# Two stages of a fused token model, their edge woven on one core: the last attention turns run together with the first mixing rounds

## The chip, the cores and the metric

One core of a Trainium2 chip (trn2). The time of a kernel is device microseconds of one launch, the median of several runs. The profile comes from one further execution, recorded by the hardware profiler.

## What is computed

128 images of 224x224 become 64 tokens of width 64 each (a two-level Haar transform, a resize, a linear layer); 32 text tokens are put behind them, which makes 96 tokens per image. Then four residual blocks follow, each on a layer-normed input. Cut to what matters:

```
h = concat([tok(x), txt], axis=1)                    # 128 x 96 x 64
h = h + gated_attention(layernorm(h))                # stage A
h = h + expert_attention(layernorm(h))               # stage B
h = h + mixing(layernorm(h))                         # stage C
h = h + routed_experts(layernorm(h))                 # stage D (routing) and E (experts)

# stage B: 4 heads x 4 expert queries of width 16 over shared keys and values
s   = einsum('bnesd,bntd->bnest', q, k) * 4 + causal
qkv = einsum('bnest,bntd->bnesd', softmax(s), v)     # zeroed where the head input is 0
gs  = softmax(out @ gate_w + gate_b)                 # weights of the 4 experts
hn  = layernorm16(sum_e gs * qkv + resid)
hx  = layernorm16(fc2(relu(fc1(hn))) + hn)           # rows of width 16
out = hx * softmax(hx @ fgate_w)                     # one weight per head

# stage C: k, v, r = ln(x) @ Wk, Wv, Wr
y = wkv(w/T, u/T, k, v)                              # a scan along the 96 tokens
x = x + sigmoid(r) * y @ Wo
x = x + sigmoid(ln(x) @ Wr2) * (relu(ln(x) @ Wk2)**2 @ Wv2)
```

Everything is float32 apart from a few masks.

## The kernel before

It is written engine by engine: each engine has its own instruction stream, executed strictly in its order, and semaphores tie the streams together. All activations of all images stay on chip in `H` (96 tokens on the partitions, 128 x 64 columns), so that no stage around the change moves data in or out; the DMA share there is 0.

**Stages and turns.** Stage B takes the images in NG = 32 groups of G = 4. Stage C takes them in NR = 16 rounds of GD = 8, so round r needs the groups 2r and 2r+1 of stage B. Both are software pipelines written out with `grouped(eng, n, *stages)` (line 68): each entry of the list is a pair (lag, function), and in turn t an engine issues each function for group t - lag, in the order of the list. The last turns of stage B, 32 to 37 (there are up to 6 lags), have fewer and fewer entries: the run-out. The code uses `u`, the turn's buffer, beside `g`, the group.

**The edge.** TensorE, ScalarE, VectorE and GpSimd each end stage B and then wait for `b_h` = 32, the semaphore that VectorE raises when a group's residual has been added to `H` (line 1604). So no engine begins stage C before the last group of stage B is done. VectorE then sets constants (`c_decay` and borders, lines 1619 to 1627) and begins round 0.

**Stage B's late steps of a group**, in the order of dependence: `b_outs` (VectorE, lines 1504 and 1508), `b_pads` (GpSimd, 1278), `b_outT` (TensorE, 708), `b_outF` (ScalarE), `b_gates` (TensorE, 719), `b_gate1` (VectorE, 1516), `b_gexp` (ScalarE, 1065), `b_gate2` (VectorE), `b_weigh` (GpSimd, 1285), `b_mix` and `b_center1` (VectorE, 1541 to 1531), `b_squares1` (ScalarE, 1083), `b_var1` (VectorE, 1534), `b_pow1` (GpSimd, 1291), `b_hns` (VectorE, 1557), `b_fx` (TensorE), `b_fxFs` (ScalarE), `b_fc1s` (TensorE, 730), `b_reluF` (ScalarE, 1091), `b_h1s` (VectorE, 1562), `b_fc2s` (TensorE, 734), `b_ys` (VectorE, 1568), `b_yTs` (TensorE), `b_center2` (VectorE, 1529 to 1531), `b_squares2` (ScalarE, 1087), `b_var2` (VectorE, 1534), `b_pow2` (GpSimd, 1295), `b_fos` (VectorE, 1585 to 1587), `b_foTs` (TensorE), `b_foFs` (ScalarE), `b_fgates` (TensorE, 747), `b_w1` (VectorE, 1593), `b_wexp` (ScalarE, 1079), `b_w2` (VectorE, 1599 to 1604).

**Stage C's steps of a round**: `c_ln` (VectorE, 1645 to 1647), `c_squares` (ScalarE, 1113), `c_var` (VectorE, 1652), `c_power` (GpSimd, 1311), `c_scale1` (ScalarE, eight pieces, recorded at the helper's line 1006), `c_norm` (VectorE, 1659), `c_transpose` (TensorE, 770), `c_features` (ScalarE, 1006), `c_kvr` (TensorE, 790 to 793), `c_kvs` (ScalarE, 1006 and 1134), `c_wkv1` (VectorE, 1669 to 1673), `c_exps` (ScalarE, 1139 to 1144), `c_wkv2` (VectorE, 1684 to 1694), `c_out` (TensorE, 799), `c_resid` (VectorE, 1700 to 1710), then the second norm, the hidden layer, `c_values` (TensorE, 838) and `c_end` (VectorE, 1727 to 1729). The lags run from 0 to 4; stage C's rounds 0 to 7 are written out, 8 to 15 run in a hardware loop.

**Memory.** PSUM has 8 banks, and each stage names its own: before, stage B has the scores in 0 and 1, the turned scores (`T0_`) in 2 and 3, outputs 4 (`O_`), features 5 (`F_`), queries and gates 6 (`Q_`), the small layers 7 (`Z_`). Stage C uses all eight in the order of its names. The on-chip tiles of both stages are cut from one `arena`, where they lie on top of each other, and from `XR`.

Of the kernel before, what the change touches and what calls it, by code (L numbers as in the profile page):

```python
# [111 lines left out]
def build(nc, t_in, table, mpe, out):  # L112
    ctx = ExitStack()
    with ctx:  # L114
# [112 lines left out]
        gst = tb("gst", [NTOK, 4, G * NH])
        gd = tb("gd", [NTOK, G * NM])
        ge = tb("ge", [NTOK, G * NM])
        gs = tb("gs", [NTOK, G * NM])  # L230
# [1 line left out]
        hm = tb("hm", [NTOK, GC])
        hc = tb("hc", [NTOK, GC])
        hs = tb("hs", [NTOK, GC])
        hn = tb("hn", [NTOK, GC])
        hst = tb("hst", [NTOK, 4, G * NH])
        hcy = tb("hcy", [NTOK, GC])
        hsy = tb("hsy", [NTOK, GC])
        hsty = tb("hsty", [NTOK, 4, G * NH])
        gsty = tb("gsty", [NTOK, 4, G * NH])  # L240
        gdy = tb("gdy", [NTOK, G * NH])
        gey = tb("gey", [NTOK, G * NH])
        fxF = tb("fxF", [P, FC])
        pmF = tb("pmF", [P, FC])
        h1 = tb("h1", [P, FC])
        yF = tb("yF", [P, FC])
        fo = tb("fo", [NTOK, GC])
        foF = tb("foF", [P, FC])
        assert tb.at <= 14592
# [1769 lines left out]
```

## Time and profile before

| | us |
|---|---|
| median of 3 runs | 2515.45 (2511.88 to 2518.7) |
| the profiled execution | 2491.33 |
| its span in the profile | 2489.3 |

Busy shares of the span and instructions:

| engine | busy us | share | instructions |
|---|---|---|---|
| TensorE, matmuls | 1906.3 | 77% | 16407 |
| VectorE | 1609.2 | 65% | 5040 |
| ScalarE | 976.9 | 39% | 3150 |
| GpSimd | 1045.3 | 42% | 878 |

The page cuts the span in 40 slices of 62.2 us. The expert attention, stage B, ends in slice 24 and stage C in slice 29; the images and stage A lie before, the routing and the experts behind. Slices 23 and 24 hold the edge between stage B and stage C. The profiled execution is 24 us shorter than the median of the runs: differences are read within one trace, and set against its own time.

How the rows below are read: a line of the timeline is one instruction or several merged ones: start in us from the span's start, duration in us, engine, source line, operation, what it writes and reads, the shape; in brackets the idle time of the engine before it and who ended it. PE is TensorE, DVE VectorE, ACT ScalarE, POOL GpSimd. A row of windows gives, for a stretch, its length, then busy us (and number of instructions) of PE, of PE's weight loads, of DVE, ACT and POOL, then the granted TensorE clock as a share of full speed.

### The profile page before, as it was taken

What the parts mean: (1) busy time and instruction counts of PE and PEld (TensorE: products, weight loads), DVE (VectorE), ACT (ScalarE), POOL (GpSimd) and SP (SyncE); (2) the same over time, 40 slices, a digit from 0 to 9 for tenths busy, and PEclk for the clock granted to TensorE, in tenths of its full rate; (3) what the DMA queues carried; (4) which work ended last, traced back from release to release, by engine and by line L of the source; (5) the groups of instructions that cost most, each with busy time, mean ns of one, the idle gap of its engine ahead of it and who ended that gap; (6) DMA issues with size and microseconds to landing.
All of it is one profiled execution on the core that took longest, in us unless ns stands there. A gap on an engine that the chain in (4) does not pass through costs nothing. (4 is left out here: it accounts for less than half of the span.)

```text
span 2489.3 us, 52573 instructions
## 1 busy us (share of the span) xinstructions
PE 1906.3 (77%) x16407; PEld 1481.9 (60%) x16407; DVE 1609.2 (65%) x5040; ACT 976.9 (39%) x3150; POOL 1045.3 (42%) x878
## 2 busy tenths in 40 slices
PE   5778887899999999999999527677533332998970
PEld 2256666677777777777777415556422222887860
DVE  0035564368888888888888559999588873333223
ACT  2366664234444444444444247877322210111100
POOL 0033342023443443444433422222178784777772
PEclk9989998689999999999999557777655555555555
DMA  9910000000000000000000000000000003665526
GB/s 283 299 46 0 0 0 0 1 2 2 2 1 0 0 0 0 0 0 0 0 0 1 1 0 1 1 0 0 0 21 22 23 22 92 180 166 146 159 81 160
DMA packets 119877, 106.63 MB, mean 43 GB/s; under 512 B 62448, under 2 KB 109680, under 8 KB 118896
## 3 DMA queue, kind: packets, MB, share of 16 engines
q1 hardware_dynamic: 87024, 73.88, 11.3%
q10 hardware_dynamic: 18432, 16.79, 2.3%
q0 software_dynamic: 14336, 14.91, 1.8%
q8 instruction: 45, 0.74, 0.1%
q14 instruction: 40, 0.33, 0.0%
HBM read 78.84 MB, written 26.67 MB: 42 GB/s over the span
## 5 line engine op out<-in xcount | busy, mean ns | idle before, releaser
L1006 ACT ACTIVATE arena<-PS 128x384 f32<-128x384 f32 (+3 forms) x384 | 178.5, 483 | 570.6 <-DMA arena<-in_t_experts_dram 212.2
L1354 POOL DMA_INDIRECT expert_rows<-arena x256 | 248.4, 970 | 104.0 <-issue 77.5
L1489 DVE TENSOR_REDUCE XR<-PS 128x2 f32<-128x192 f32 (+2 forms) x768 | 173.7, 280 | 105.0 <-PE PS L645 104.8
L645 PE MATMUL PS<-arena 32*128 32x96 f32 (+2 forms) x3072 | 234.1, 285 | 0.0
L1341 POOL DMA_INDIRECT routed_rows<-XR,SLu x192 | 201.5, 1049 | 74.9 <-issue 67.3
L645 PEld LDWEIGHTS PS<-arena 32*128 32x128 f32 x3072 | 198.4, 192 | 20.7
L1042 ACT ACTIVATE XR<-PS 128x256 f32<-128x256 f32 x512 | 167.3, 380 | 67.2 <-PE PS L660 66.9
L1295 POOL TENSOR_TENSOR arena<-arena,mhalf 96x16 f32<-96x16 f32 x32 | 92.7, 2898 | 225.8 <-DVE arena L1535 225.8
L1493 DVE TENSOR_TENSOR XR<-PS,XR 128x192 f32<-128x192 f32 (+2 forms) x768 | 172.4, 278 | 0.0
L612 PE MATMUL PS<-arena,WP 128*128 128x192 f32 x640 | 151.4, 361 | 18.4 <-ACT arena L1006 17.8
L660 PE MATMUL PS<-WP,XR 128*128 128x128 f32 (+1 forms) x1024 | 163.7, 284 | 1.0 <-ACT XR L1042 1.0
L679 PE MATMUL PS<-XR,arena 96*32 96x128 f32 (+2 forms) x3072 | 148.7, 288 | 6.6 <-DVE arena L1508 5.1
L1285 POOL TENSOR_TENSOR arena<-arena 96x1024 f32<-96x1024 f32 x32 | 61.7, 1929 | 194.0 <-DVE arena L1525 194.0
L917 PEld LDWEIGHTS PS<-arena 128*128 128x128 f32 x512 | 114.0, 328 | 46.9 <-DVE arena L1852 42.2
L1006 ACT ACTIVATE XR<-PS 128x384 f32<-128x384 f32 (+1 forms) x144 | 75.8, 526 | 167.4 <-PE PS L679 167.4
L917 PE MATMUL PS<-arena 128*128 128x64 f32 x512 | 126.0, 428 | 20.0 <-DVE arena L1852 19.7
L909 PE MATMUL PS<-arena 65*128 65x128 f32 x512 | 129.4, 434 | 2.8 <-ACT arena L1006 2.8
L1257 POOL TENSOR_TENSOR arena<-arena 128x384 f32<-128x384 f32 x64 | 73.9, 1174 | 134.6 <-ACT arena L975 134.6
L612 PEld LDWEIGHTS PS<-arena,WP 128*128 128x128 f32 x640 | 105.6, 199 | 34.7 <-ACT arena L1006 19.6
L1269 POOL TENSOR_TENSOR rstd<-stat,mhalf 96x4 f32<-96x4 f32 x32 | 36.2, 1131 | 203.5 <-DVE stat L1462 184.4
L660 PEld LDWEIGHTS PS<-WP,XR 128*128 128x128 f32 (+1 forms) x1024 | 115.1, 130 | 9.5 <-DVE XR L1493 1.6
L909 PEld LDWEIGHTS PS<-arena 65*128 65x128 f32 x512 | 116.8, 333 | 3.2 <-ACT arena L1006 3.2
(304 smaller groups left out, 4542.7 us busy)
## 6 DMA issues: line engine op xcount, KB each, us to landing
arena<-in_x_dram SPq DMA_DIRECT2D x32, 784.0 KB, 9.9
arena<-in_t_experts_dram ACTq DMA_DIRECT2D x128, 128.0 KB
arena<-in_t_experts_dram SPq DMA_DIRECT2D x128, 128.0 KB
routed_rows<-zt SPq DMA_DIRECT2D x16, 528.0 KB, 6.1
arena<-routed_rows SPq DMA_DIRECT2D x64, 132.0 KB
expert_rows<-arena POOLq DMA_INDIRECT x256
WP<-in_t_pack_dram SPq DMA_DIRECT2D x1, 3425.0 KB, 20.6
routed_rows<-XR,SLu POOLq DMA_INDIRECT x192, 2.2
```

The lines of the kernel that those rows point to most:

```text
L612: mm = pe.matmul(o, w[:, par, :], sxF[:, u, :].rearrange("p (q t) -> p q t", q=2), start=True, stop=True)
L645: mm = pe.matmul(PS[:, i, S_AT[j]:S_AT[j] + QB * (j + 1)], qF[rows, u, 3 * b + j, :], kF[rows, u, keys], start=False, stop=True, skip_grou ...
L660: mm = pe.transpose(PS[0:keys, T0_ + i, n * P:(n + 1) * P], Pe[:, p, i, n * P:n * P + keys], ident[:, :])
L679: mm = pe.matmul(PS[32 * n:32 * n + 32, O_, j * P:(j + 1) * P], Vx[rows, u, b * NH + n, :], PT[rows, b % 2, n, at:at + P], start=True, sto ...
L909: mm = pe.matmul(PS[:, 2 + u % 2, k * SLOT:(k + 1) * SLOT], wx[0:D + 1, u, k, 0:NHX], xT[:, u % 2, k * SLOT:(k + 1) * SLOT], start=True, s ...
L917: mm = pe.matmul(PS[:, 4 + u % 2, k * D:(k + 1) * D], hT[:, u % 2, k * SLOT:(k + 1) * SLOT], wx[:, u, k, NHX:NHX + D], start=True, stop=True)
L1006: return act.activation(dst, src, ACT.Identity, **kw)
L1042: act.activation(PT[:, b % 2, 2 * p + i, :], bank(T0_ + i, P, 2 * P), ACT.Exp).then_inc(b_exp, 1)
L1341: pool.indirect_dma_start(XD, bass.IndirectOffsetOnAxis(SLu[:, u, k, b:b + 1], 0), XG[:, u, b, k, :], None).then_inc(scat[u], 16)
L1354: pool.indirect_dma_start(YD, bass.IndirectOffsetOnAxis(yi[:, u % 4, k:k + 1], 0), yb[:, u % 4, k, :], None).then_inc(e_st[u % 2], 16)
L1489: dve.tensor_reduce(negmax[:, p, j, :], PS[:, 0:2, S_AT[j]:S_AT[j] + QB * (j + 1)], AX_X, ALU.max, negate=True).then_inc(b_max, 1)
L1493: dve.tensor_tensor(Pe[:, p, :, P_AT[j]:P_AT[j] + QB * (j + 1)], PS[:, 0:2, S_AT[j]:S_AT[j] + QB * (j + 1)], negmax[:, p, j, :].unsqueeze( ...
```

## The change

`grouped` gets a first turn and an end, and a new helper `part` issues a piece of a turn's list. Each engine's list of stage B is named (`b_order`), the pipeline stops early, and the last turns are issued in pieces, with pieces of the rounds 0, 1 and 2 of stage C between them. From turn 3 of stage C the old list runs on. VectorE keeps turns up to 34 whole and weaves 35 to 37; TensorE and ScalarE weave from 33 on, GpSimd from 35 on. The full wait for `b_h` = 32 goes on ScalarE and GpSimd, becomes `b_h` = 29 on VectorE, and stands on TensorE behind turn 2 of stage C. Waits that it covered are written out (`b_s`, `b_gate`, `b_o`, `b_om`, `b_av`, `b_exp`, `b_sub`, `b_vx`, `b_pad`, `tab_set`).

For both stages to run at once, tiles and banks become disjoint. In the arena, stage C keeps 0 up, stage B's early tiles move to 8704 up, its late ones (`tl`) to 16560 up; `M1` moves to `XR`. Stage B's banks become `F_` 0, `Q_` 1, `T0_` 2 and 3, `O_` 4, scores (`S_`) 5 and 6, `Z_` 7; stage C's `T_`, `K_`, `V_`, `R_`, `OO`, `K0`, `K1`, `VV` become 0, 2, 3, 5, 4, 6, 7, 1. No instruction's shape changes, and each is issued as often as before.

```diff
-def grouped(eng, n, *stages, unroll=2):
+def grouped(eng, n, *stages, unroll=2, start=0, stop=None):
...
-    for t in range(lo):
+    for t in range(start, lo):
...
-    for t in range(n, n + lmax):
+    for t in range(n, n + lmax if stop is None else stop):
         step(t, 0, n)
+
+def part(n, t, *stages, unroll=2):
+    for lag, stage in stages:
+        if 0 <= t - lag < n:
+            stage(t - lag, (t - lag) % unroll)
...
-        t0, ta, tb, tc, td = (Arena(arena) for _ in range(5))
+        t0, ta, tb, tl, tc, td = (Arena(arena) for _ in range(6))
+        tb.at, tl.at = 8704, 16560
...
-        M1 = tb("M1", [NTOK, G * NM * DH])
+        M1 = tx("M1", [NTOK, G * NM * DH])
...
-            T0_, O_, F_, Q_, Z_ = 2, 4, 5, 6, 7
+            F_, Q_, T0_, O_, S_, Z_ = 0, 1, 2, 4, 5, 7
...
-            pe.wait_ge(b_h, NG)
-            T_, K_, V_, R_, OO, K0, K1, VV = range(8)
+            T_, K_, V_, R_, OO, K0, K1, VV = 0, 2, 3, 5, 4, 6, 7, 1
...
+            grouped(pe, NG, *b_order, stop=NG + 1)
...
+            fc1_at, foT_at = b_order.index((4, b_fc1s)), b_order.index((4, b_foTs))
+            part(NG, NG + 1, *b_order)
+            pe.wait_ge(b_vx, NG)
+            pe.wait_ge(b_pad, NG)
+            pe.wait_ge(b_exp, 4 * G * NG)
+            pe.wait_ge(b_sub, 6 * G * NG)
+            part(NG, NG + 2, *b_order[:fc1_at])
+            part(NR, 0, (0, c_transpose), unroll=4)
+            part(NG, NG + 2, *b_order[fc1_at:foT_at])
+            part(NR, 0, (0, c_kvr), unroll=4)
+            part(NG, NG + 2, *b_order[foT_at:])
+            part(NG, NG + 3, *b_order[:fc1_at])
+            part(NR, 1, (0, c_transpose), unroll=4)
+            part(NG, NG + 3, *b_order[fc1_at:foT_at])
+            pe.wait_ge(b_o, G * NG)
+            part(NR, 1, (0, c_kvr), (1, c_out), unroll=4)
+            part(NG, NG + 3, *b_order[foT_at:])
+            part(NG, NG + 4, *b_order)
+            part(NR, 2, *c_order, unroll=4)
+            pe.wait_ge(b_h, NG)
+            grouped(pe, NR, *c_order, unroll=4, start=3)
...
-            act.wait_ge(b_h, NG)
-            act.wait_ge(tab_set, 3)
+            grouped(act, NG, *b_order, stop=NG + 1)
...
+            part(NG, NG + 1, *b_order[:foF_at])
+            act.wait_ge(b_s, 2 * G * NG)
+            act.wait_ge(tab_set, 3)
+            part(NR, 0, (0, c_squares), unroll=4)
+            part(NG, NG + 1, *b_order[foF_at:fxF_at])
+            part(NR, 0, (0, c_scale1), unroll=4)
+            part(NG, NG + 1, *b_order[fxF_at:])
+            part(NG, NG + 2, *b_order[:gexp_at + 1])
+            part(NR, 0, (0, c_features), unroll=4)
+            part(NG, NG + 2, *b_order[gexp_at + 1:foF_at])
+            act.wait_ge(b_gate, NG)
+            part(NR, 0, (0, c_kvs), unroll=4)
+            part(NR, 1, (0, c_squares), (1, c_exps), unroll=4)
+            part(NG, NG + 2, *b_order[foF_at:wexp_at])
+            part(NR, 1, (0, c_scale1), unroll=4)
+            part(NG, NG + 2, *b_order[wexp_at:])
+            part(NR, 1, (0, c_features), unroll=4)
+            part(NG, NG + 3, *b_order[:foF_at])
+            part(NR, 1, (0, c_kvs), unroll=4)
+            part(NR, 2, (0, c_squares), (1, c_exps), unroll=4)
+            part(NG, NG + 3, *b_order[foF_at:])
+            part(NR, 2, (0, c_scale1), (2, c_squares2), (0, c_features), (0, c_kvs), unroll=4)
+            grouped(act, NR, *c_order, unroll=4, start=3)
...
-            pool.wait_ge(b_h, NG)
+            grouped(pool, NG, *b_order, stop=NG + 3)
...
+            part(NG, NG + 3, *b_order[:weigh_at])
+            part(NR, 0, (0, c_power), unroll=4)
+            part(NG, NG + 3, *b_order[weigh_at:])
+            part(NG, NG + 4, *b_order[:weigh_at])
+            part(NR, 1, (0, c_power), unroll=4)
+            part(NG, NG + 4, *b_order[weigh_at:])
+            part(NR, 2, (0, c_power), unroll=4)
+            grouped(pool, NR, *c_order, unroll=4, start=3)
...
-            dve.wait_ge(b_h, NG)
+            grouped(dve, NG, *b_order, stop=NG + 3)
+            dve.wait_ge(b_h, NG - 3)
+            dve.wait_ge(b_av, G * NG)
...
+            part(NR, 0, (0, c_ln), unroll=4)
+            part(NG, NG + 3, *b_order[:hn_at])
+            part(NR, 0, (0, c_var), unroll=4)
+            part(NG, NG + 3, *b_order[hn_at:h1_at])
+            part(NR, 0, (0, c_norm), unroll=4)
+            part(NG, NG + 3, *b_order[h1_at:])
+            part(NR, 1, (0, c_ln), unroll=4)
+            part(NG, NG + 4, *b_order[:fo_at])
+            dve.wait_ge(b_om, G * NG)
+            part(NR, 1, (1, c_wkv1), unroll=4)
+            part(NG, NG + 4, *b_order[fo_at:hn_at])
+            part(NR, 1, (0, c_var), unroll=4)
+            part(NG, NG + 4, *b_order[hn_at:h1_at])
+            part(NR, 1, (0, c_norm), unroll=4)
+            part(NG, NG + 4, *b_order[h1_at:])
+            part(NR, 1, (1, c_wkv2), unroll=4)
+            part(NR, 2, (0, c_ln), unroll=4)
+            part(NG, NG + 5, *b_order[:fo_at])
+            part(NR, 2, (1, c_wkv1), unroll=4)
+            part(NG, NG + 5, *b_order[fo_at:hn_at])
+            part(NR, 2, (0, c_var), unroll=4)
+            part(NG, NG + 5, *b_order[hn_at:])
+            part(NR, 2, (2, c_resid), (0, c_norm), (1, c_wkv2), (2, c_var2s), unroll=4)
+            grouped(dve, NR, *c_order, unroll=4, start=3)
```

The lists themselves, which are only named in the change, stand in the functions above.

## Rows read from the trace of the kernel before

**Rows 1.** Windows: stretch, length, busy us per engine, clock, DMA share, GB/s
```profile
1401.65:1450.25 48.60, 15.07 (x60) 10.26 (x60) 23.55 (x70) 6.37 (x18) 18.76 (x9) 0.50 0.00 0
1450.25:1497.66 47.41, 16.28 (x38) 8.28 (x38) 31.23 (x53) 24.70 (x105) 8.69 (x3) 0.58 0.00 0
1497.66:1717.00 219.34, 159.64 (x904) 125.85 (x904) 206.93 (x311) 177.87 (x637) 54.39 (x24) 0.73 0.00 1
```

**Rows 2.** Timeline of VectorE, attention turns 34 to 37: start, length, instruction [idle before]
```profile
1401.23 0.42 DVE L1531 TENSOR_TENSOR arena<-PS,arena 96x256 f32<-96x256 f32 x1
1402.14 0.42 DVE L1534 TENSOR_REDUCE arena<-arena 96x16 f32<-96x256 f32 x1 [0.48 <-ACT arena L1087]
...
1415.97 0.22 DVE L1516 TENSOR_REDUCE arena<-PS 96x16 f32<-96x64 f32 x1 [1.80 <-PE PS L719]
...
1418.35 0.26 DVE L1562 TENSOR_SCALAR arena<-arena 128x192 f32<-128x192 f32 x1 [1.91 <-ACT arena L1091]
...
1425.09 0.42 DVE L1531 TENSOR_TENSOR arena<-PS,arena 96x256 f32<-96x256 f32 x1
1425.99 0.42 DVE L1534 TENSOR_REDUCE arena<-arena 96x16 f32<-96x256 f32 x1 [0.48 <-ACT arena L1087]
...
1429.62 0.43 DVE L1585 TENSOR_TENSOR arena<-arena 96x256 f32<-96x256 f32 x1 [2.48 <-POOL arena L1295]
...
1432.86 0.17 DVE L1593 TENSOR_REDUCE arena<-PS 96x4 f32<-96x16 f32 x1 [1.90 <-PE PS L747]
...
1436.31 0.26 DVE L1562 TENSOR_SCALAR arena<-arena 128x192 f32<-128x192 f32 x1 [1.29 <-ACT arena L1091]
...
1440.29 0.42 DVE L1531 TENSOR_TENSOR arena<-PS,arena 96x256 f32<-96x256 f32 x1
...
1449.79 0.42 DVE L1604 TENSOR_TENSOR H<-H,arena 96x256 f32<-96x256 f32 x1
```

**Rows 3.** Timeline of VectorE, mixing rounds 0 to 3
```profile
1452.85 0.69 DVE L1647 TENSOR_TENSOR arena<-H,arena 96x512 f32<-96x512 f32 x1
...
1467.17 0.97 DVE L1669 TENSOR_TENSOR_SCAN arena<-arena 128x388 f32<-128x388 f32 x1 [5.95 <-ACT arena L1134]
...
1473.09 0.95 DVE L1684 TENSOR_TENSOR XR<-XR,arena 128x768 f32<-128x768 f32 x1
...
1481.57 0.68 DVE L1645 TENSOR_REDUCE arena<-H 96x8 f32<-96x512 f32 x1
...
1485.40 0.68 DVE L1700 SCALAR_TENSOR_TENSOR arena<-PS,arena 96x512 f32<-96x512 f32 x1
...
1488.50 0.69 DVE L1659 TENSOR_TENSOR arena<-arena 96x512 f32<-96x512 f32 x1 [0.78 <-POOL arena L1311]
...
1497.66 0.67 DVE L1645 TENSOR_REDUCE arena<-H 96x8 f32<-96x512 f32 x1
```

**Rows 4.** Timeline of GpSimd (POOL), the same stretch
```profile
1410.29 0.71 POOL L1278 TENSOR_TENSOR arena<-arena 96x256 f32<-96x256 f32 x1
...
1429.55 2.90 POOL L1291 TENSOR_TENSOR arena<-arena,mhalf 96x16 f32<-96x16 f32 x1
...
1456.08 2.90 POOL L1311 TENSOR_TENSOR arena<-arena,mhalf 96x16 f32<-96x16 f32 x1 [11.29 <-issue]
```

**Rows 5.** Timeline of ScalarE (ACT), mixing rounds 0 and 1
```profile
1459.01 2.02 ACT L1006 ACTIVATE arena<-arena 96x64 f32<-96x64 f32 x8 [3.34 <-POOL arena L1311]
...
1469.35 0.84 ACT L1139 ACTIVATE arena<-arena 128x768 f32<-128x768 f32 x1 [0.33 <-DVE arena L1673]
...
1470.96 1.49 ACT L1144 ACTIVATE XR<-arena 128x1536 f32<-128x1536 f32 x1
```

**Rows 6.** Timeline of TensorE (PE), turns 32 and 34, round 0
```profile
1361.17 0.59 PE L730 MATMUL PS<-arena,WP 128*128 128x192 f32 x2
...
1416.85 1.01 PE L730 MATMUL PS<-arena,WP 128*128 128x192 f32 x2 [0.60 <-ACT arena L1006]
...
1459.80 0.87 PE L770 MATMUL PS<-WP,arena 96*128 96x96 f32 x4 [11.77 <-issue]
```

More of the change, by code:

```diff
@@ L224, in build @@
         oden = tb("oden", [NTOK, NM])
-        OT = tb("OT", [NTOK, 2, G, NM * DH])
+        OT = tl("OT", [NTOK, 2, G, NM * DH])
         OF = tb("OF", [P, 2 * G, NTOK])
[L227 to L230, printed above, removed]
-        M1 = tb("M1", [NTOK, G * NM * DH])
[L232 to L249, printed above, removed]
+        gst = tl("gst", [NTOK, 4, G * NH])
+        gd = tl("gd", [NTOK, G * NM])
+        ge = tl("ge", [NTOK, G * NM])
+        gs = tl("gs", [NTOK, G * NM])
+        M1 = tx("M1", [NTOK, G * NM * DH])
+        hm = tl("hm", [NTOK, GC])
+        hc = tl("hc", [NTOK, GC])
+        hs = tl("hs", [NTOK, GC])
+        hn = tl("hn", [NTOK, GC])
+        hst = tl("hst", [NTOK, 4, G * NH])
+        hcy = tl("hcy", [NTOK, GC])
+        hsy = tl("hsy", [NTOK, GC])
+        hsty = tl("hsty", [NTOK, 4, G * NH])
+        gsty = tl("gsty", [NTOK, 4, G * NH])
+        gdy = tl("gdy", [NTOK, G * NH])
+        gey = tl("gey", [NTOK, G * NH])
+        fxF = tl("fxF", [P, FC])
+        pmF = tl("pmF", [P, FC])
+        h1 = tl("h1", [P, FC])
+        yF = tl("yF", [P, FC])
+        fo = tl("fo", [NTOK, GC])
+        foF = tl("foF", [P, FC])
+        assert ta.at <= 8704 and tb.at <= 14592 and tabs.at <= 16560
         tcx = Arena(XR)
@@ L273, in build @@
         r2S = tc("r2S", [NTOK, GDC])
+        assert tc.at <= 16560
         EX = tcx("EX", [P, 6, GD // 2, WD])
@@ L644, in stage @@
                             rows = slice(32 * (2 * p + i), 32 * (2 * p + i) + 32)
-                            mm = pe.matmul(PS[:, i, S_AT[j]:S_AT[j] + QB * (j + 1)], qF[rows, u, 3 * b + j, :],
+                            mm = pe.matmul(PS[:, S_ + i, S_AT[j]:S_AT[j] + QB * (j + 1)], qF[rows, u, 3 * b + j, :],
                                            kF[rows, u, keys], start=False, stop=True, skip_group_check=True)
@@ L1170, in c_relu2 @@
                 return stage
-            grouped(act, NR, (0, c_squares), (1, c_exps), (3, c_features2), (0, c_scale1), (2, c_squares2), (0, c_features),
-                    (3, c_relu2(0)), (0, c_kvs), (3, c_relu2(1)), unroll=4)
+            c_order = ((0, c_squares), (1, c_exps), (3, c_features2), (0, c_scale1), (2, c_squares2), (0, c_features),
+                    (3, c_relu2(0)), (0, c_kvs), (3, c_relu2(1)))
+            gexp_at, foF_at, fxF_at = b_order.index((3, b_gexp)), b_order.index((4, b_foFs)), b_order.index((3, b_fxFs))
+            wexp_at = b_order.index((4, b_wexp))
+            part(NG, NG + 1, *b_order[:foF_at])
[21 more added lines that the diff above has]
+            grouped(act, NR, *c_order, unroll=4, start=3)
             act.wait_ge(c_h, NR)
@@ L1316, in c_power2 @@
                 pool.tensor_tensor(cst2[:, u % 2, 4, :], cst2[:, u % 2, 3, :], mhalf[0:NTOK, 0:GD], ALU.pow).then_inc(n2_rstd, 1)
-            grouped(pool, NR, (3, c_power2), (0, c_power), unroll=4)
+            c_order = ((3, c_power2), (0, c_power))
+            weigh_at = b_order.index((4, b_weigh))
+            part(NG, NG + 3, *b_order[:weigh_at])
[6 more added lines that the diff above has]
+            grouped(pool, NR, *c_order, unroll=4, start=3)
             pool.wait_ge(c_h, NR)
@@ L1730, in c_end @@
                 dve.sem_inc(c_h, 1)
-            grouped(dve, NR, (0, c_ln), (1, c_wkv1), (3, c_norm2), (0, c_var), (2, c_resid), (4, c_end), (0, c_norm), (1, c_wkv2),
-                    (2, c_var2s), unroll=4)
+            c_order = ((0, c_ln), (1, c_wkv1), (3, c_norm2), (0, c_var), (2, c_resid), (4, c_end), (0, c_norm), (1, c_wkv2),
+                    (2, c_var2s))
+            fo_at, hn_at, h1_at = b_order.index((6, b_fos)), b_order.index((5, b_hns)), b_order.index((5, b_h1s))
+            part(NR, 0, (0, c_ln), unroll=4)
[22 more added lines that the diff above has]
+            grouped(dve, NR, *c_order, unroll=4, start=3)
             dve.wait_ge(c_h, NR)
```

38 lines of the change are left out of this document (17 added, 21 removed).

## The prediction

> **What bounds the kernel now.** The page's busy shares (TensorE 77%, VectorE 65%) are means over stages with different limits, so I read its 40 slices first. Two stages matter. In the expert attention TensorE is full. In the mixing stage VectorE is: 206.93 of 219.34 us from round 3's start on [rows 1]. Between them lie some 96 us in which no engine is full. Next I cut those at two marks of VectorE's timeline: the end of its attention turn 34, at 1401.23 + 0.42 = 1401.65, and the end of turn 37, at 1449.79 + 0.42 = 1450.21 [rows 2]. Mixing round 3 starts at 1497.66 [rows 3]. From 1401.65 to there is 96.0 us, in which VectorE works 23.55 + 31.23 = 54.8 us; TensorE's granted clock is 0.50, then 0.58 of full, so mostly its lower level, 1.2 GHz [rows 1]. The rest is one chain of steps, each waiting for another engine. Turn 35 takes 23.9 us, turn 36 15.2 and turn 37 9.5 (ends of consecutive turns, [rows 2]), rounds 0 to 2 with the constants 47.4.
>
> The change keeps VectorE's work and lets the mixing rounds fill the waits of the attention turns. VectorE's attention order is untouched through turn 34, and from round 3 on the mixing order is the old one. So the question is where round 3 starts. The floor is 1401.65 + 54.8 = 1456.4, a gain of 41 us; the dependences decide how much of it is reached.
>
> **The change, part by part.** I follow the new order by hand, taking distances between instructions from the old rows. Times below are in the old trace's scale.
>
> *The constants and round 0's sums come ahead of turn 35.* From the end of L1604 to the end of L1647 is 1453.54 - 1450.21 = 3.3 us [rows 2, 3]. So the sums end at 1404.95, and the first instruction of turn 35, which stood at 1402.14 because it waited for ScalarE [rows 2], starts 2.8 us later. ScalarE was idle here: round 0's squares end near 1407 and nobody waits.
>
> *GpSimd.* It takes pow2(29), pads(1), (2), pow1(30) and pads(3) in the old order, 2.8 later; pads(3) ended at 1410.29 + 0.71 = 1411.0 and now ends at 1413.8. c_power(0) follows: 2.90 as in L1311 [rows 4], to 1416.7. The weights' product b_weigh(31) behind it is not ready until 1423.7, so this is hidden.
>
> *Gate.* b_gate1(31) stood at 1415.97 and stands at 1418.8: its feed runs through pads(3), a transpose, ScalarE's copy and the gate matmuls, all 2.8 later. ScalarE's c_scale1(0) (2.02, [rows 5]) runs from 1416.7 to 1418.75, ahead of the copy b_fxFs(30), which is ready only at 1419.1: hidden, with 0.3 to spare.
>
> *Round 0's transpose ahead of b_fc1(30).* The old distance from gate1 to h1s(30) is 1418.35 - 1415.97 = 2.4 [rows 2]. Now there stand between them: gate1 0.5, c_norm(0) 0.65, the transpose 0.87, fc1 1.01 [rows 6], relu 0.45, together 3.4 with hand-overs. The shift grows to 3.85. The rest of turn 35 is as before, so it ends at 1425.09 + 0.42 + 3.85 = 1429.35. TensorE then has b_yTs(30) behind it and runs the three projections of c_kvr(0), 4.2 us, from 1426.4 to 1430.6; ScalarE's copies end at 1431.95. Both in time for what follows.
>
> *Turn 36.* VectorE: c_ln(1) 1.6 (0.68 + 0.2 + 0.69), to 1430.95; the two variances 1.05, to 1432.0; c_wkv1(0), 1469.35 - 1467.17 = 2.15, to 1434.15 [rows 3, 5]. ScalarE: c_exps(0), 1469.35 to 1470.96 + 1.49 = 3.1 [rows 5], to 1437.3. The fos(30) group waits for pow2(30) (its input at 1431.65, 2.90 long) and ends at 1435.95, and its transpose at 1436.5, so b_foFs(30), queued behind c_exps(0) on ScalarE, loses 0.75. Copy, gate matmul and w1 add 1.6 (the old w1 starts 1432.86 after a fos group that starts 1429.62, [rows 2], less 1.34 for fos and 0.65 for its transpose), to 1438.85. Then c_var(1), 0.25, to 1439.1; GpSimd's c_power(1) 2.90 and a hop of 0.1, to 1442.1; ScalarE's c_scale1(1) 2.02, to 1444.1. **Here is the dearest queue of the change:** the small exponential b_wexp(30) stands behind c_scale1(1), and w2(30) and c_norm(1) behind that. w2(30) 1.5 and the exponential 0.2, to 1445.8; c_norm(1) 0.65; transpose 0.9; b_fc1(31) 1.0, for TensorE has c_transpose(1) ahead of it; relu and hops 0.5: h1s(31) at 1448.85, where it was at 1436.31. From there to the turn's end the old distance holds, 1440.29 + 0.42 - 1436.31 = 4.4 [rows 2]: 1453.25. So this turn takes 23.9 us where it took 15.2.
>
> *Turn 37.* c_wkv2(0), 1481.57 - 1473.09 = 8.5 [rows 3], to 1461.75; c_ln(2) 1.6, to 1463.35; var2(31) 0.5, to 1463.85; c_wkv1(1) 2.15, to 1466.0; its exponentials to 1469.1, again ahead of b_foFs(31), whose transpose is ready at 1468.9 (pow2(31) ends at 1466.9): 0.2 lost. Copy, gate matmul, w1: 1470.65. c_var(2) and w2(31), with its exponential, to 1472.45. Here c_power(2), 1471.0 to 1473.9, is hidden behind c_resid(0). From c_resid to the start of the next c_ln the old distance is 1497.66 - 1485.40 = 12.25, of which 0.78 was a wait for GpSimd [rows 3] that is gone: 11.5. Round 3 starts at 1483.9.
>
> **Sum.** 1497.66 - 1483.9 = 13.8 us. VectorE is then 54.8 busy of 82.3. What is late next is the same chain, now through c_scale1(1) and the doubled turn 36. From round 3 on VectorE bounds as before, and projections and squares of round 2 are ready by my times (copies at 1484.8 against the 1485.4 at which they are wanted), so nothing is given back.
>
> *At no cost:* the renumbered PSUM banks and moved tiles. No instruction's shape or count changes; the two DMA-bound ends and the later stages are untouched. Nothing in the trace prices a bank number or an address; I take 0 and bound it below as the slower rival. For the added wait instructions the nearest row is a hand-over of about 0.1 us; most are long satisfied.
>
> *A rule that speaks against.* The added c_powers lie beside VectorE's two-input instructions. L1585, two inputs in the arena, starts at 1429.62, 0.07 after GpSimd's L1291 of 2.90 us, and takes 0.43 [rows 2, 4]: a pow does not hold VectorE up. The Trainium skill, "SBUF — State Buffer", section "Who interferes with whom", says that such a pair contends for a shared read interface, by an exclusive lock for the whole instruction. By that rule L1585 would have waited for 2.8 us; the trace disagrees for this kind of instruction.
>
> The profiled execution took 2491.33 us (span 2489.3), 24 us under the median of the timed runs, 2515.45. I take the gain as 13.8/2491.3 = 0.55% of the median: 2515.45 x 0.99446 = 2501.5.
>
> **Rivals.**
> - *A. The forecast*, 13.8 us, 2501.5; its own range is 2496 to 2505, since each of some 35 hand-overs may be 0.1 off.
> - *B. The pows lock VectorE out.* c_power(2) runs beside w2(31) and c_resid(0), and its 2.90 then goes onto the path: a gain of 10.9, 2504.5. Against: L1585 above.
> - *C. The denser stretch lifts TensorE's clock.* TensorE's 15.07 us in the run-out [rows 1] lie at 0.50, nearly all on the chain. L730 takes 0.59 at the full clock and 1.01 at half [rows 6], so up to 15 x 0.42 = 6 us more: 19.8, 2495.5. Against: the clock stays at 0.50 through the whole run-out at 31% busy, and with the rounds' 16.28 [rows 1] TensorE would be busy 31 of 82 us, 38%, still far from full; the rounds by themselves (34%) had 0.58. The Trainium skill, "TensorE: Matmul & The Clock Gate", section "HAM oscillation — how this bites in real kernels", says that idle gaps put the clock back; the row agrees (0.50).
> - *D. It weaves, but the strict queues give the gain back.* Orders written by hand interlock: if c_squares, c_kvs or c_scale1 meets its input late by as little as 2 us in each of the three turns, everything queued behind (b_foFs, b_wexp, b_fc1s) moves. 3 x 2 to 3 x 3 us leave a gain of 5 to 8, taken as 6: 2509.4. For: twice in my times the slack is under 0.4 us (b_fxFs(30) above, and the squares of round 1, which end at 1434.0 just ahead of c_exps(0)).
> - *E. Slower.* Banks or addresses cost something in the attention's full stretch (TensorE near full): F_ and Q_ in banks 0 and 1, scores in 5 and 6, M1 in XR. The place is the 32 turns; 0.43 us a turn eats the gain, 0.67 makes the kernel slower by 0.3%. At 0.8 it is 25.6 - 13.8 = 12 us slower: 2527.5. Against: shapes and partners stay, and each bank is still written and read under the same semaphores.
> - *F. No effect*, the weave not taking place: would need a wait on the last b_h ahead of c_ln(0). VectorE's is for b_h 29, done near 1390, and TensorE's full one stands ahead of round 3 only. In D's number.
>
> **How the numbers follow.** A 0.58, B 0.08, C 0.10, D with F 0.18, E 0.06. A change of 0.3% (7.5 us) is about what a measurement of this kernel can tell from none. A, B and C lie beyond it, less a little for a median that is off: faster 0.75. D and that little: same 0.19. E: slower 0.06. The range reaches from C with 2 us more, 2493, to past D, 2511: it leaves out E and half of the tails.
>
> **What would show it.** In the new profile: c_ln(0)'s reduce right behind turn 34; the two L1534 of turn 35 some 2.8 us later; b_wexp(30) behind eight c_scale1 pieces; no waiting of VectorE in c_wkv2(0); the stretch from the end of turn 34 to round 3's c_ln 82 us instead of 96; the attention's turn before it and the mixing rounds after it of the old length. I am wrong if the turns before 34 change length, if VectorE waits in round 3, or if the woven turns 35 and 36 are far from 27.7 and 23.9 us.

## The result and the profile after

The changed kernel is faster by about 0.6%: medians 2498.78 us (2474.35 to 2515.47) against 2514.81 (2494.67 to 2534.13), 18 runs each, ratio 0.9938 with a 95% interval of 0.9915 to 0.9961. The ratio leaves out the runs that lie more than 1.5% above the fastest of the same kernel. Forecast was 2501.5 and a gain of 0.55%. The profiled execution took 2474.35 us, 17.0 less than that of before.

The windows of the changed kernel, cut at the ends of VectorE's turns 34, 35 and 36 and at round 3's `c_ln`, then the stretch as a whole, and behind it a piece of the mixing stage as long as the third of [rows 1]. The columns are those of [rows 1]:

```profile
1399.34:1426.68 27.34, 12.58 (x49) 9.21 (x50) 16.67 (x51) 7.92 (x34) 13.12 (x7) 0.50 0.00 1
1426.68:1449.98 23.30, 7.19 (x23) 4.05 (x22) 10.90 (x32) 10.76 (x37) 8.76 (x3) 0.57 0.00 0
1449.98:1480.80 30.82, 10.06 (x29) 5.96 (x27) 26.35 (x43) 13.04 (x53) 6.38 (x2) 0.59 0.00 0
1399.34:1480.80 81.46, 29.84 (x98) 19.22 (x98) 53.93 (x123) 31.72 (x124) 28.26 (x12) 0.56 0.00 0
1480.80:1700.14 219.34, 156.25 (x909) 123.26 (x910) 207.39 (x312) 178.93 (x636) 54.87 (x25) 0.76 0.00 1
```

The two rows of before, 48.60 and 47.41 us [rows 1], have become one of 81.46, with the same work: VectorE's 23.55 + 31.23 = 54.8 us are now 53.93. The clock has hardly moved: 0.56, where the whole stretch had 0.54 before and its two parts 0.50 and 0.58 [rows 1]. The last row's length is chosen and shows nothing of the rounds' time. The `c_ln` that ended the third row of before, at 1717.00, starts here at 1699.46:

```profile
1699.46 0.67 DVE L1706 TENSOR_REDUCE arena<-H 96x8 f32 x1
```

So the rounds 3 and on took 218.66 us to that point, 0.7 less than the 219.34 of before. From here on "the stretch" is this distance, end of turn 34 to round 3's `c_ln`: 96.01 us before, 81.46 after.

VectorE's timeline of the changed kernel at the marks of [rows 2, 3]. L1591 ends an attention turn's centring, L1706 begins a `c_ln`, L1622 is `b_h1s`, L1653 `b_w1`, L1659 `b_w2`, L1720 `c_norm`, L1745 the start of `c_wkv2`:

```profile
1398.92 0.42 DVE L1591 TENSOR_TENSOR arena<-PS,arena 96x256 f32<-96x256 f32 x1
...
1400.95 0.68 DVE L1706 TENSOR_REDUCE arena<-H 96x8 f32<-96x512 f32 x1
...
1402.48 0.41 DVE L1594 TENSOR_REDUCE arena<-arena 96x16 f32<-96x256 f32 x1
...
1419.53 0.26 DVE L1622 TENSOR_SCALAR arena<-arena 128x192 f32<-128x192 f32 x1 [2.14 <-ACT arena L1120]
...
1426.26 0.42 DVE L1591 TENSOR_TENSOR arena<-PS,arena 96x256 f32<-96x256 f32 x1
...
1435.56 0.17 DVE L1653 TENSOR_REDUCE arena<-PS 96x4 f32<-96x16 f32 x1 [2.48 <-PE PS L756]
...
1441.35 0.17 DVE L1659 TENSOR_REDUCE arena<-arena 96x4 f32<-96x16 f32 x1 [4.95 <-ACT arena L1108]
...
1442.76 0.68 DVE L1720 TENSOR_TENSOR arena<-arena 96x512 f32<-96x512 f32 x1
...
1445.59 0.26 DVE L1622 TENSOR_SCALAR arena<-arena 128x192 f32<-128x192 f32 x1 [2.14 <-ACT arena L1120]
...
1449.56 0.42 DVE L1591 TENSOR_TENSOR arena<-PS,arena 96x256 f32<-96x256 f32 x1
1449.90 0.94 DVE L1745 TENSOR_TENSOR XR<-XR,arena 128x768 f32<-128x768 f32 x1
...
1458.38 0.67 DVE L1706 TENSOR_REDUCE arena<-H 96x8 f32<-96x512 f32 x1
...
1480.80 0.67 DVE L1706 TENSOR_REDUCE arena<-H 96x8 f32<-96x512 f32 x1
```

The waits in brackets are to be read first. The 5.95 us for the first copies of k and v [rows 3] are gone. The longest is now 4.95, ahead of `b_w2(30)`, for L1108, ScalarE's 0.2 us exponential. ScalarE's timeline says why:

```profile
1434.35 0.31 ACT L1035 ACTIVATE arena<-PS 128x192 f32<-128x192 f32 x1
1439.20 2.02 ACT L1035 ACTIVATE arena<-arena 96x64 f32<-96x64 f32 x8 [4.54 <-POOL arena L1362]
1441.12 0.20 ACT L1108 ACTIVATE arena<-arena 96x16 f32<-96x16 f32 x1
```

The eight pieces of `c_scale1(1)` wait for GpSimd's power, and the exponential, whose input was there at 1435.9, stands behind them.

### The profile page after: what moved, and what is told of

The parts are those of the page before. It is cut to its first block and busy times, and to the rows that moved or that the text cites. A ratio compares the mean times of both kernels' runs of the same rounds, so it can differ in the third digit from the quotient of the medians.

```text
span 2472.2 us, 52578 instructions
## 1 busy us (share of the span) xinstructions
PE 1911.1 (77%) x16407; PEld 1490.3 (60%) x16407; DVE 1608.0 (65%) x5040; ACT 977.7 (40%) x3150; POOL 1044.0 (42%) x878
## 5 line engine op out<-in xcount | busy, mean ns | idle before, releaser
L1337 POOL TENSOR_TENSOR XR<-arena 96x1024 f32<-96x1024 f32 x32 | 61.7, 1929 | 191.8 <-DVE arena L1585 191.8
```

## The experiments

The time of one kernel spreads by 1.6% over 18 runs, while the stretch is the same to a few hundredths: 81.46 and 81.47 us in two profiles of the changed kernel, 95.99 and 96.01 in two kernels with the old order. So what each edit is worth is read from the stretch. The ratios of times, with intervals of 6 to 9 us to either side, only bound what might be lost elsewhere. Each ratio is to the kernel before on the same chip; its median was 2592.38 us beside the first three experiments and the first with fillers, 2594.6 beside the second with fillers, and 2512.74 beside the others. They differ by up to 82 us, so times are compared on one chip only.

### Disjoint tiles and renumbered banks alone

```diff
-            grouped(pe, NG, *b_order, stop=NG + 1)
+            grouped(pe, NG, *b_order)
+            pe.wait_ge(b_h, NG)
...
+            grouped(pe, NR, *c_order, unroll=4)
```

The same on the other engines: the changed kernel's placement with the old orders and waits.

> The disjoint tiles and the renumbered banks of the changed kernel, with the old orders and the old full waits for b_h: nothing is woven. My theory (banks and addresses are free, all of the gain is the weave): from the end of attention turn 34 to round 3's c_ln 96.0 us as before, attention turns of 28.8 us, time ratio to the kernel before 1.000 within 0.002. Rival (the placement itself gives or costs something): turns of stage B off by 0.1 us or more, or an edge other than 96 us, and a ratio outside 0.998 to 1.002; if half of the measured gain were the placement's, the ratio would be 0.997.

VectorE's timeline of this kernel; L1543 ends turn 34, L1657 begins round 3:

```profile
1415.38 0.42 DVE L1543 TENSOR_TENSOR arena<-PS,arena 96x256 f32<-96x256 f32 x1
...
1511.79 0.67 DVE L1657 TENSOR_REDUCE arena<-H 96x8 f32<-96x512 f32 x1
```

1511.79 - 1415.80 = 95.99 us, and the last full turns have 28.7 us here and in the kernel before. From the first residual of stage B to the end of turn 34 it is 820.5 us in both, so the 28 or so turns between agree to less than 0.1 us in all. The ratio is 1.0023 (0.9999 to 1.0046), whose middle lies just outside the stated 0.998 to 1.002, on the slow side; the interval takes in 1. The placement gives nothing, so the whole gain of the stretch is the weave's.

### Only round 0 woven

```diff
             part(NG, NG + 3, *b_order[h1_at:])
-            part(NR, 1, (0, c_ln), unroll=4)
-            part(NG, NG + 4, *b_order[:fo_at])
+            part(NG, NG + 4, *b_order)
+            part(NG, NG + 5, *b_order)
             dve.wait_ge(b_om, G * NG)
...
-            grouped(dve, NR, *c_order, unroll=4, start=3)
+            grouped(dve, NR, *c_order, unroll=4, start=1)
```

VectorE's part, against the changed kernel; between the last lines all other pieces of rounds 1 and 2 and of turns 36 and 37 go. The other engines likewise.

> Only mixing round 0 is woven into the run-out; rounds 1 and 2 follow behind it in the old order. My theory (round 0's chain of waits is what the weave hides, above all VectorE's wait for the first copies of k and v; rounds 1 and 2 had few waits to give): turn 35 27.3 us, turns 36 and 37 24.7 as in the kernel before, then c_ln(1) to c_ln(3) 38.0 less the 6.0 of that wait, 32.1, so 84 us from the end of turn 34 to round 3's c_ln, where the changed kernel has 81.5 and the one before 96.0. Rival (each round hides its share): a third of the 14.5 us gained, so 91 us.

The stretch is 84.07 us, 84 by my reading and 91 by an equal share of each round; ratio 0.9971 (0.9948 to 0.9993). 11.9 of the 14.5 us come from round 0. Rounds 1 and 2 together add 2.6. The parts came as foretold: turn 35 took 27.3 us, turns 36 and 37 to `c_ln(1)` 24.6, and from there to round 3's `c_ln` it was 32.1. One thing lies outside the stretch: turn 34, just ahead of it, took 31.9 us in this profile and 29.8 to 30.1 in the other kernels with the same turn. Its granted clock was 0.54 against 0.61 before, and VectorE's and TensorE's instructions up to there are those of the changed kernel, so I put it down to chance; no run tested that.

### The small exponential ahead of the scaling

```diff
-            part(NG, NG + 2, *b_order[foF_at:wexp_at])
+            part(NG, NG + 2, *b_order[foF_at:wexp_at + 1])
             part(NR, 1, (0, c_scale1), unroll=4)
-            part(NG, NG + 2, *b_order[wexp_at:])
+            part(NG, NG + 2, *b_order[wexp_at + 1:])
```

> The changed kernel with one exchange on ScalarE: b_wexp(30), a 0.2 us exponential, is issued ahead of round 1's c_scale1 and not behind it. My theory (VectorE's 4.95 us wait before w2(30) is that queue, and c_norm(1) then waits for c_power(1) only): w2(30) right after w1(30) and b_hns(31), c_norm(1) at 1439.2 where it was at 1442.8, but b_fxFs(31) is still behind c_scale1(1), so h1s(31) some 2.4 us earlier: 79.0 us from the end of turn 34 to round 3's c_ln, against 81.5. Rival (that wait hides another that takes its place): 81.5 within 0.5.

Waits of VectorE in this kernel's turn 36:

```profile
1455.75 0.17 DVE L1653 TENSOR_REDUCE arena<-PS 96x4 f32<-96x16 f32 x1 [2.48 <-PE PS L756]
...
1459.39 0.69 DVE L1720 TENSOR_TENSOR arena<-arena 96x512 f32<-96x512 f32 x1 [1.39 <-POOL arena L1362]
...
1463.36 0.26 DVE L1622 TENSOR_SCALAR arena<-arena 128x192 f32<-128x192 f32 x1 [3.28 <-ACT arena L1120]
```

The 4.95 us are gone. 1.39 have come back as a wait for the power itself, and the wait for the relu has grown from 2.14 to 3.28, since the copy for `b_fc1s(31)` is still behind the scaling. Net 2.4: a stretch of 79.07, foretold 79.0. Ratio 0.9960 (0.9937 to 0.9983).

### A doubled power, for the step called hidden

```diff
+                if isinstance(g, int) and g == 0:
+                    pool.tensor_tensor(sq[0:NTOK, 0, 0:2 * GD], cvar[:, u % 2, :], mhalf[0:NTOK, 0:2 * GD], ALU.pow)
```

> The changed kernel with c_power(0) issued twice on GpSimd (the first result goes to a buffer that nobody reads): 2.9 us more ahead of c_norm(0) and c_scale1(0), which I called hidden, the latter with little to spare. My theory: c_norm(0) moves by 0.65 and b_fc1s(30), behind b_fxFs(30), which is queued behind c_scale1(0), by 1.7 us: 83.2 us from the end of turn 34 to round 3's c_ln. Rival 1 (there is slack behind it): 81.5. Rival 2 (the power is wholly on the chain, or holds VectorE up by a lock of the port): 84.4 or more.

This kernel ran once, for its profile, so its time isn't compared. Two waits of VectorE in turn 35:

```profile
1448.72 0.69 DVE L1722 TENSOR_TENSOR arena<-arena 96x512 f32<-96x512 f32 x1 [0.56 <-POOL arena L1364]
...
1452.68 0.26 DVE L1624 TENSOR_SCALAR arena<-arena 128x192 f32<-128x192 f32 x1 [3.27 <-ACT arena L1120]
```

`c_norm(0)` waits 0.56 where it didn't wait, and `b_h1s(30)` 3.27 where it waited 2.14. The stretch is 83.27 us, foretold 83.2. So 2.9 us more on GpSimd cost 1.8: the power was hidden, with some 1.1 us to spare, and not by a wide margin. At the place that the prediction named it was less. The copy `b_fxFs(30)`, behind `c_scale1(0)`, came 2.65 us later in its turn, so about 0.25 was spare there (0.3 by the prediction); the rest lies behind it, where `b_fc1s(30)` stood behind `c_transpose(0)` on TensorE anyway.

### TensorE kept busy

```diff
+            def fill(n):
+                for _ in range(n):
+                    pe.matmul(PS[:, 6, 0:P], ident[:, :], ident[:, :], start=True, stop=True)
...
+            fill(20)
+            part(NG, NG + 1, *b_order[foT_at:])
```

And so at five more places.

> The changed kernel with 81 extra matmuls of 128x128 on the identity, into a bank that nobody reads in that stretch, placed on TensorE where it waits longest in the woven turns (20 ahead of b_foTs(29), 12 behind c_kvr(0), 14 ahead of c_transpose(1), 14 and 11 around c_out(0), 10 behind b_fgates(31)): work added only to keep TensorE busy. My theory (TensorE's steps of the chain are at the lower clock, and worth up to 6 us): the granted clock of the stretch goes from 0.56 to 0.8 or more, L728 from 2.82 to 1.6, and the stretch from 81.5 to 76 to 78 us. Rival 1 (the clock doesn't follow): 0.56 as before and the stretch 81.5 to 85, longer by the fillers that overrun their gaps. Rival 2 (TensorE's steps aren't on the chain): the clock rises and the stretch stays at 81.5.

TensorE in this kernel: the gate matmuls of turn 35, `b_fc1s(30)` and `b_fc2s(30)`, then `b_fc1s(31)` and `b_fc2s(31)`:

```profile
1430.71 2.82 PE L728 MATMUL PS<-WP,arena 128*96 128x64 f32 x16
...
1435.39 0.90 PE L739 MATMUL PS<-arena,WP 128*128 128x192 f32 x2
...
1437.49 1.00 PE L743 MATMUL PS<-arena,WP 128*128 128x192 f32 x2 [1.20 <-DVE arena L1638]
...
1461.15 0.52 PE L739 MATMUL PS<-arena,WP 128*128 128x192 f32 x2
...
1463.08 0.59 PE L743 MATMUL PS<-arena,WP 128*128 128x192 f32 x2 [1.41 <-DVE arena L1638]
```

The mean granted clock of the stretch rose from 0.56 to 0.72, but turn 35 took its 27.34 us as before. Turn 36, where the groups took 0.52 and 0.59 us, gave 0.9 us, and what follows 0.5. The stretch is 80.10, 1.4 us shorter, with whatever the fillers cost by standing in the queue already in it. My 76 to 78 was a miss, and so were L728 at 1.6 and a clock of 0.8. Neither rival fits whole: the clock did follow in part, and some of the steps are on the chain. Ratio 0.9941 (0.9914 to 0.9967).

With more fillers in turn 35:

```diff
-            fill(20)
+            fill(36)
...
+            part(NG, NG + 2, *b_order[:1])
+            fill(3)
+            part(NG, NG + 2, *b_order[1:fc1_at])
+            fill(2)
...
```

This is against the kernel just shown; 3 and 5 more fillers stand behind `b_fc1s(30)` and `b_fc2s(30)`.

> As fill_clock, with more of the same extra matmuls in turn 35, where the first one left the clock at its lower level: 36 ahead of b_foTs(29) and 2 to 5 in each of the short waits behind b_fgates(29), b_fx(30), b_fc1s(30) and b_fc2s(30). fill_clock lifted the clock in turns 36 and 37 only and took 1.4 us off. My theory now: if L728 runs at the full clock (1.6 for 2.8), turn 35's TensorE steps give 3.3 us more, and the stretch from the end of turn 34 to round 3's c_ln is 76.8 us. Rival 1 (turn 35's steps have slack behind them, as VectorE waits for GpSimd and ScalarE there too): 79 to 80 with L728 at 1.6. Rival 2 (the clock of turn 35 isn't lifted by this much work either): L728 stays at 2.8 and the stretch at 80 to 81, or longer by what the fillers overrun.

```profile
1416.02 9.11 PE L858 MATMUL PS<-WP 128*128 128x128 f32 x72
1427.33 0.38 PE L585 MATMUL PS<-WP,arena 96*128 96x96 f32 x2 [2.20 <-DVE arena L1669]
...
1428.22 0.78 PE L756 MATMUL PS<-WP,arena 128*96 128x8 f32 x4 [0.18 <-ACT arena L1057]
...
1432.37 2.82 PE L728 MATMUL PS<-WP,arena 128*96 128x64 f32 x16
...
1439.15 0.59 PE L743 MATMUL PS<-arena,WP 128*128 128x192 f32 x2 [0.26 <-DVE arena L1645]
```

```profile
1440.23 1.75 DVE L1651 TENSOR_TENSOR arena<-arena 128x192 f32<-128x192 f32 x1
```

Rival 2: after 9 us of fillers (L858, two records for each) and 2 us of idling the first transpose still ran at the full clock (0.38 against 0.58). The granted clock was 0.97 from 1427.3 to 1428.2 and 0.50 from there on, and L728 again took 2.82. Stretch 80.09 us, ratio 0.9953 (0.9929 to 0.9976). `b_fc2s(30)`, L743, did run at the full clock (0.59), and VectorE no longer waited for it. That gained nothing: the next of its instructions, L1651 of `b_ys`, took 1.75 us where it had taken 1.33, since it lies beside GpSimd's product (last section), and turn 35 had 27.34 us again. What the full clock at L728 would be worth is left open: neither filling raised it there.

### Another interlacing

The same pieces of work in another order, found by laying VectorE's work without waits over the others' chains. On VectorE:

```diff
             part(NG, NG + 4, *b_order[hn_at:h1_at])
+            part(NR, 1, (1, c_wkv2), unroll=4)
+            part(NG, NG + 4, (5, b_h1s))
             part(NR, 1, (0, c_norm), unroll=4)
-            part(NG, NG + 4, *b_order[h1_at:])
-            part(NR, 1, (1, c_wkv2), unroll=4)
+            part(NG, NG + 4, (5, b_ys), (5, b_center2))
             part(NR, 2, (0, c_ln), unroll=4)
-            part(NG, NG + 5, *b_order[:fo_at])
-            part(NR, 2, (1, c_wkv1), unroll=4)
-            part(NG, NG + 5, *b_order[fo_at:hn_at])
-            part(NR, 2, (0, c_var), unroll=4)
-            part(NG, NG + 5, *b_order[hn_at:])
-            part(NR, 2, (2, c_resid), (0, c_norm), (1, c_wkv2), (2, c_var2s), unroll=4)
+            part(NG, NG + 5, (6, b_var2))
+            part(NR, 2, (0, c_var), (1, c_wkv1), unroll=4)
+            part(NG, NG + 5, (6, b_fos))
+            part(NR, 2, (2, c_resid), (0, c_norm), unroll=4)
+            part(NG, NG + 5, (6, b_w1))
+            part(NR, 2, (1, c_wkv2), unroll=4)
+            part(NG, NG + 5, (6, b_w2))
+            part(NR, 2, (2, c_var2s), unroll=4)
```

Beside it the changed kernel ran once more.

> The changed kernel itself, beside the next two on one chip, so that they can be set against it. Every theory: the time ratio to the kernel before of its first measurement, 0.994 within 0.003, and 81.5 us from the end of turn 34 to round 3's c_ln.

> The changed kernel with another interlacing of turns 36 and 37 with rounds 0 to 2, same work: c_wkv2(0), 8.6 us of VectorE without a wait, stands ahead of b_h1s(31), so that GpSimd, ScalarE and TensorE do c_power(1), c_scale1(1), b_fx(31), b_fc1(31) and b_reluF(31) behind it; b_wexp(30) and b_fxFs(31) go ahead of c_scale1(1), c_transpose(1) behind b_fc2s(31), b_fos(31) and c_resid(0) into the wait for round 1's exponentials, b_w2(31) behind c_wkv2(1). c_resid gets a semaphore of its own, so that it needn't stand behind w2(31). My theory (the changed kernel's stretch is bound by waits at the seams, not by VectorE's 54 us of work): 73.3 us from the end of turn 34 to round 3's c_ln, against 81.5; 0.3% less than the changed kernel. Rival (the chain through b_fos(31) and b_w2(31) is the bound whatever stands between): 80 to 82.

The main waits of VectorE in turns 36 and 37 of this kernel; L1630 is `b_ys(31)`, L1591 its centring, L1715 `c_var(2)`, L1732 `c_wkv1(1)`:

```profile
1458.99 0.17 DVE L1655 TENSOR_REDUCE arena<-PS 96x4 f32<-96x16 f32 x1 [2.47 <-PE PS L756]
...
1471.39 0.42 DVE L1630 SCALAR_TENSOR_TENSOR arena<-PS,WP,arena 128x192 f32<-128x192 f32 x1 [0.51 <-PE PS L743]
1472.96 0.42 DVE L1591 TENSOR_REDUCE arena<-PS 96x16 f32<-96x256 f32 x1 [0.76 <-PE PS L592]
1477.64 0.17 DVE L1715 TENSOR_SCALAR arena<-arena 96x8 f32<-96x8 f32 x1 [1.55 <-ACT arena L1141]
1478.76 0.97 DVE L1732 TENSOR_TENSOR_SCAN arena<-arena 128x388 f32<-128x388 f32 x1 [0.88 <-ACT arena L1162]
1485.15 0.17 DVE L1655 TENSOR_REDUCE arena<-PS 96x4 f32<-96x16 f32 x1 [0.16 <-PE PS L756]
```

The 4.95 us and turn 36's wait of 2.14 are gone. What is left there is short but for the 2.47 us ahead of `b_w1(30)`, which were there before. Turn 35's waits are those of the changed kernel. The stretch is 72.62 us (foretold 73.3), with VectorE 53.76 busy. The repeated changed kernel had 81.47. Times: this kernel 0.9877 of the one before (0.9852 to 0.9901), the changed one beside it 0.9918 (0.9887 to 0.9949); medians 2485.91 and 2496.05. The intervals of the two overlap, so that it beats the changed kernel is shown by the stretch, not by the times alone; that it beats the kernel before is shown by both.

> As weave2a, and two pieces of VectorE's work go into waits of turn 35: the constants into the 1.87 us for pow2(29), and c_ln(1) into the 2.14 us for b_reluF(30). My theory: both are wholly hidden, 1.6 us each, so 70.1 us from the end of turn 34 to round 3's c_ln, and 0.45% less time than the changed kernel. Rival (what depends on them starts earlier but the exchange delays b_h1s(30) and b_fos(29) as much): no less than 72.5.

Against the kernel just shown, the decay constants, which stood at the start of the stretch on VectorE, ahead of `c_ln(0)`, are moved into the wait ahead of `b_fos(30)`, and `c_ln(1)` goes ahead of `b_h1s`:

```diff
-            link = Link(dve, c_tab, 0, 5)
...
-            dve.wait_ge(tab_set, 3)
...
-            part(NG, NG + 3, *b_order[:hn_at])
+            part(NG, NG + 3, *b_order[:fo_at])
+            link = Link(dve, c_tab, 0, 5)
+            link(dve.memset(c_decay[:, :, :].rearrange("p q w -> p (q w)"), 0.0))
...
+            dve.wait_ge(tab_set, 3)
+            part(NG, NG + 3, *b_order[fo_at:hn_at])
...
             part(NR, 0, (0, c_norm), unroll=4)
+            part(NR, 1, (0, c_ln), unroll=4)
             part(NG, NG + 3, *b_order[h1_at:])
-            part(NR, 1, (0, c_ln), unroll=4)
```

```profile
1399.95 0.86 DVE L1647 TENSOR_TENSOR arena<-arena 96x256 f32<-96x256 f32 x1 [0.37 <-POOL arena L1349]
...
1413.31 0.26 DVE L1624 TENSOR_SCALAR arena<-arena 128x192 f32<-128x192 f32 x1 [0.62 <-ACT arena L1121]
...
1420.94 0.42 DVE L1596 TENSOR_REDUCE arena<-arena 96x16 f32<-96x256 f32 x1 [0.48 <-ACT arena L1117]
1422.88 0.97 DVE L1720 TENSOR_TENSOR_SCAN arena<-arena 128x388 f32<-128x388 f32 x1 [0.79 <-ACT arena L1162]
...
1429.27 0.17 DVE L1655 TENSOR_REDUCE arena<-PS 96x4 f32<-96x16 f32 x1 [2.98 <-PE PS L756]
```

Both pieces went into their waits, which shrank from 1.87 to 0.37 and from 2.14 to 0.62. But 0.48 and 0.79 us came back where `c_ln(1)` had stood as cover, ahead of `b_var2(30)` and `c_wkv1(0)`, and 0.5 more ahead of `b_w1(30)`, while the 0.43 ahead of `b_fos(30)` went: 3.4 saved and 1.8 given back. The stretch is 70.88 us where I said 70.1; ratio 0.9907 (0.9872 to 0.9942). Between these last two the times can't choose.

## Why the prediction was right

- **The floor and the bound.** VectorE's work was to stay (54.8, measured 53.93) and the dependences to decide. They did: 27.5 of 81.5 us are still waits.
- **Turn by turn.** Turn 35 with constants: 27.7 said, 27.34 measured. Turn 36: 23.9 and 23.30. From there to round 3: 30.65 and 30.82. Sum 82.25 and 81.46; gain 13.8 and 14.55 us.
- **The terms that were off.** I added the whole 0.87 of `c_transpose(0)` and the whole 1.01 of `b_fc1s(30)`. The second starts 0.70 after the first (1417.44 and 1418.14): merged rows of TensorE overlap, and the start-to-start distance is what counts. That made the way from `b_gate1` to `b_h1s` 0.2 shorter. Another 0.15 of turn 35's 0.36 came ahead of it: the first L1594 stands 2.65 later in its turn, not 2.8. Turn 36 gave 0.6, of which 0.25 by the same two steps and the rest in small pieces ahead of `c_norm(1)`. The last piece was 0.2 longer. There GpSimd's pow2(31) took 3.49 us instead of 2.90 (below), and ScalarE sat idle 0.42 for the transpose that hangs on it; small gains elsewhere took back half. In all the sum was 0.8 us too long.
- **The dearest queue** was named ahead, with its place. The exchange of two instructions (79.07) and the new interlacing (72.62) show that it was real and that it was a choice of order.
- **Rival B, the lock.** The added powers did not hold VectorE up; in the changed kernel `c_resid(0)` follows `b_w2(31)` without a gap beside `c_power(2)`, and each takes what it took before.
- **Rival C, the clock.** It stayed low: 0.56, and 0.52 in the repeat, whose stretch was as long (81.47). Had it risen, up to 6 us was my price; the part that fillers could raise was worth 1.4. For L728 in turn 35 it is not settled.
- **Rival D, the strict queues.** They cost 2.4 us at one place and some 9 in all against the better interlacing, but my hand-made order contained that cost already.
- **Rival E, the placement.** 95.99 us with the new banks and tiles alone, and the attention turns ahead of it as long as before, where the rival needed 0.43 us a turn. The time's interval alone would still allow 0.46% slower.
- **The whole time.** The profiled span shrank by 17.1 us, of which 14.55 in the stretch. 1.3 lie ahead of the first residual of stage B, which came at 581.2 us before and at 579.9 after. This part varies by itself: in the repeat of the same changed kernel it came at 607.7. 1.0 lies between that residual and the end of turn 34 (820.45 and 819.44). A changed length ahead of turn 34 was one of my signs of being wrong, but the repeat had 820.47, so it isn't the change's. From round 3's `c_ln` to the end it was 991.6 and 991.4, and 996.4 in the repeat. So that the two profiled spans agree this well outside the stretch is luck. The ratio's 0.62% is the stretch's 0.58% of the span within its interval, and that interval, 0.39 to 0.85%, is wide: it is the stretch that confirms the sum, and the whole time only doesn't contradict it.

## What to carry to other kernels

Where one engine is the bound of the stage that follows, the edge between two stages is worth at most its length less that engine's own work (here 41 us, of which the change reached 14.55 and the best order tried 25). How much of it is reached can be worked out from start-to-start distances in the old trace, turn by turn, if every in-order queue is followed. In this kernel the first woven round gave most, 11.9 us, about 6 of them the wait for the first k and v. After that look for a short instruction that others wait for behind a long wait in its queue, and put the bound engine's longest piece without waits (here the 8.6 us of `c_wkv2`) over the others' longest chain.

## What was not expected of the hardware

VectorE and GpSimd hold each other up, but not with every kind of instruction. Four pairs of the changed kernel, each VectorE's line and GpSimd's:

```profile
1410.68 0.69 DVE L1714 TENSOR_SCALAR arena<-arena 96x8 f32<-96x8 f32 x1
...
1421.73 1.33 DVE L1629 TENSOR_TENSOR arena<-arena 128x192 f32<-128x192 f32 x1
...
1431.73 0.43 DVE L1645 TENSOR_TENSOR arena<-arena 96x256 f32<-96x256 f32 x1 [0.42 <-POOL arena L1347]
...
1460.43 0.96 DVE L1730 TENSOR_TENSOR_SCAN arena<-arena 128x388 f32<-128x388 f32 x1
```

```profile
1410.62 0.73 POOL L1330 TENSOR_TENSOR arena<-arena 96x256 f32<-96x256 f32 x1
...
1420.92 1.93 POOL L1337 TENSOR_TENSOR XR<-arena 96x1024 f32<-96x1024 f32 x1 [6.46 <-DVE arena L1585]
...
1431.67 2.90 POOL L1343 TENSOR_TENSOR arena<-arena,mhalf 96x16 f32<-96x16 f32 x1
...
1460.59 3.49 POOL L1347 TENSOR_TENSOR arena<-arena,mhalf 96x16 f32<-96x16 f32 x1 [21.43 <-DVE arena L1595]
```

Beside a multiplication over wide rows VectorE's instruction ends when GpSimd's does: L1714, elsewhere 0.16, at 1411.37 against 1411.35; L1629, elsewhere 0.36, at 1423.06 against 1422.85. For L1629, with two inputs in the arena, this is what the Trainium skill says in "SBUF — State Buffer", section "Who interferes with whom": such an instruction contends with one of GpSimd that reads there. L1714 has one input, for which the same section names a contention only in a mode that uses both ports; which mode it ran in, the trace doesn't show. Beside a power over 16 columns the third pair shows nothing on VectorE (0.43). In the fourth, the reverse case, the power began 0.16 into VectorE's 0.96 us scan and took 3.49 instead of 2.90: 0.59 longer, with 0.80 of the scan left. Two smaller cases of the same trace go the same way. A power that began with 0.32 us of VectorE's two-input L1646 left took 3.07 (1407.58), and `c_power(1)`, with 0.25 of L1617 left, took 3.00 (1436.16); beside a reduce, with one input, it took 2.90 (1428.81). That a power reads its operands only at its start would fit all of them, but no run tested it.
